# Four-layer graph kernel on one core: layer 2 scores from stacked halves through DRAM, layer 3 attention normalised early, centred weights, and 64-column pair products

## The reference

```python
# layer 0, hypergraph convolution, twice, with relu and layer norm between them
H = (adj != 0); xw = x @ W.T
m = Be[:, :, None] * einsum('nce,nch->neh', H, xw)       # Be: 1 / column count of H
out = Dn[:, :, None] * einsum('nce,neh->nch', H, m) + b  # Dn: 1 / (H @ first row of adj)
# layer 1
agg = einsum('bij,bjd->bid', adj, k * mask)
w = mask / 16 * einsum('bid,bid->bi', q, agg)
L = softmax(w, axis=1)[:, :, None] * v
# layer 2, eight heads of 32
scores = einsum('bhqd,bhkd->bhqk', q, k) * SCALE * (adj + adj)
out = einsum('bhqk,bhkd->bhqd', softmax(scores), v) @ Wo.T + bo
# layer 3
xg = x * sigmoid(deg * Wd + bd); QK = sigmoid(xg @ Wqk.T + bqk)
scores = einsum('bnd,bmd->bnm', QK, QK) / 16 * adj
attn = scores / (scores.sum(-1) + 1e-6)
out = relu((attn @ xg) @ Wl.T + bl + xg @ Wr.T)
```

## Time and profile before

| | |
|---|---|
| median of three runs | 999.5 us (997.31 to 1002.46) |
| the profiled execution's own time | 999.49 us |
| its span, first to last instruction | 997.7 us |
| TensorE busy | 928.4 us, 93% |
| VectorE busy | 836.6 us, 84% |
| GpSimd busy | 746.0 us, 75% |
| ScalarE busy | 702.5 us, 70% |
| mean granted TensorE clock | 0.977 of full |
| DMA | 61.80 MB, 23.4% of 16 engines' span |

### The profile page before, as it was taken

One profiled execution on the slowest core, in us unless ns is written; L12 is line 12 of the kernel. 1 busy time (PEld: TensorE's weight loads), 2 busy tenths in 40 slices (PEclk: granted clock), 3 DMA queues, 4 the chain that ended last, 5 costly groups with the idle time before them and its releaser, 6 DMA issues. The chain is left out here.

```text
span 997.7 us, 32479 instructions
## 1 busy us (share of the span) xinstructions
PE 928.4 (93%) x11228; PEld 812.0 (81%) x11228; DVE 836.6 (84%) x2503; ACT 702.5 (70%) x1516; POOL 746.0 (75%) x1169
## 2 busy tenths in 40 slices
PE   4687899999999999999999999999999999999854
PEld 3566788888888888888888888888888888887642
DVE  4467888898998999899988899899989898988752
ACT  3445667777777777877787777787787777776552
POOL 2655768878878888888888888888888888876551
PEclk9779999999999999999999999999999999999995
DMA  7102221222222222222222222222222222212200
GB/s 238 40 9 60 58 68 50 56 54 61 71 71 71 56 68 53 58 61 61 71 71 71 59 66 56 56 59 65 68 71 71 63 63 67 54 37 52 52 20 21
DMA packets 110231, 61.80 MB, mean 62 GB/s; under 512 B 57072, under 2 KB 105840, under 8 KB 110192
## 3 DMA queue, kind: packets, MB, share of 16 engines
q1 hardware_dynamic: 110192, 61.30, 23.4%
HBM read 35.83 MB, written 8.39 MB: 44 GB/s over the span
## 5 line engine op out<-in xcount | busy, mean ns | idle before, releaser
L784 ACT ACTIVATE late<-preG,nbG,rsG 128x256 f32<-128x256 f32 x64 | 34.9, 592 | 63.1 <-POOL nbG L1295 63.1
L481 PE MATMUL bank<-z1h,W 128*128 128x256 f16 x256 | 72.0, 281 | 3.8 <-DVE z1l L951 3.6
L482 PE MATMUL bank<-z1l,W 128*128 128x256 f16 x256 | 72.0, 281 | 0.0
L483 PE MATMUL bank<-z1h,W 128*128 128x256 f16 x256 | 72.0, 281 | 0.0
L1374 POOL TENSOR_TENSOR late<-late,Smx 128x512 f32<-128x512 f32 x64 | 67.5, 1055 | 4.7 <-DVE Smx L1182 4.7
L481 PE MATMUL bank<-W,rFh 128*128 128x256 f16 x256 | 70.7, 276 | 0.0
L483 PE MATMUL bank<-W,rFl 128*128 128x256 f16 x256 | 70.7, 276 | 0.0
L482 PE MATMUL bank<-W,rFh 128*128 128x256 f16 x256 | 70.7, 276 | 0.0
L1300 POOL TENSOR_TENSOR gp<-late,bdb 128x512 f32<-128x512 f32 x32 | 40.7, 1271 | 32.7 <-ACT late L897 32.7
L813 ACT ACTIVATE r<-bank,b1c 128x256 f32<-128x256 f32 x128 | 52.6, 463 | 16.7 <-PE bank L483 16.7
L1283 POOL TENSOR_TENSOR y0l<-y,y0h 128x512 f16<-128x512 f32 x32 | 37.2, 1163 | 31.6 <-ACT y0h L766 31.6
(11 more groups left out here) (286 smaller groups left out, 4519.0 us busy)
## 6 DMA issues: line engine op xcount, KB each, us to landing
Vbd<-vst SPq DMA_DIRECT2D x128, 66.0 KB, 2.1
xin<-x SPq DMA_DIRECT2D x32, 256.0 KB, 2.7
xres<-x SPq DMA_DIRECT2D x32, 256.0 KB, 2.9
Kbd<-kst SPq DMA_DIRECT2D x128, 64.0 KB, 2.0
out<-late SPq DMA_DIRECT2D x32, 256.0 KB, 2.2
mrow<-mask SPq DMA_DIRECT2D x32, 128.0 KB, 3.1
atA<-adj_t SPq DMA_DIRECT2D x64, 32.0 KB, 2.3
aC<-adj SPq DMA_DIRECT2D x64, 32.0 KB, 2.1
```

The source lines that it names most:

```text
L481: pe.matmul(o, sh, mh, start=start, stop=False, skip_group_check=True)
L482: pe.matmul(o, sh, ml, start=False, stop=False, skip_group_check=True)
L483: return pe.matmul(o, sl, mh, start=False, stop=stop, skip_group_check=True)
L784: m = act.activation(dst[:, t], pre[k][:, t], ACT.Identity, bias=nb[k][:, t:t + 1], scale=rs[k][:, t:t + 1])
```

## The change

- Layer 2's scores contract over 96 rows: a head's q is stacked as (high, high, low) and its k as (high, low, high), so that one product of 64 columns per head, tile and graph gives all three parts. The stacking moves rows between partitions: q and k are written to a DRAM scratch and read back in three parts. SyncE's list gets `park_k` at the head of the step, `fetch_k` after `load_residual`, and `park_q`, `store`, `fetch_q` at the end. `Kbd` and its clearing go.
- Layer 3's attention is normalised before it meets y3: VectorE sums each row while it multiplies by adj, GpSimd scales the rows, TensorE turns the matrix, ScalarE and VectorE split it, and the bias, xg Wr and the attention product all accumulate in one bank; VectorE then takes relu and adds the residual in one instruction.
- Layers 1 and 3 compute only the diagonal 64 x 64 blocks, and `am`, the mask and `atG` are 64 columns wide.
- Wv1, Wo and bo are centred in the set-up so that two norms (C and F) have mean zero and need no mean product.
- The second half of the `rF` remainder moves from VectorE to GpSimd. All order lists are new.

```diff
-ORDER_PE = [3, 2, 1, 5, 0, 2, 4, 4, 3, 2, 5, 1, 0, 2, 0, 4, 3, 5, 0, 0, 3, 1, 5, 4, 5, 1, 3, 2, 5, 3, 1, 0, 2, 0, 4]
+ORDER_PE = [1, 2, 3, 5, 3, 0, 4, 4, 2, 1, 2, 0, 5, 4, 0, 2, 5, 3, 3, 0, 1, 0, 4, 5, 1, 2, 5, 3, 5, 2, 3, 1, 0, 0, 4]
-ORDER_ACT = [0, 5, 2, 3, 5, 1, 3, 0, 4, 5, 0, 0, 4, 4, 1, 4, 0, 5, 0, 0, 1, 0, 0, 2, 0, 3, 1, 3, 2, 5, 4, 3, 2, 4, 5]
+ORDER_ACT = [3, 1, 5, 5, 0, 2, 0, 4, 0, 3, 5, 4, 0, 4, 4, 1, 1, 0, 0, 0, 2, 5, 3, 0, 0, 2, 0, 1, 3, 4, 3, 2, 4, 5]
-ORDER_DVE = [0, 2, 0, 0, 2, 0, 0, 0, 0, 4, 1, 3, 4, 0, 4, 0, 2, 4, 4, 2, 5, 1, 0, 1, 3, 1, 5, 0, 2, 2, 2, 5, 3, 4, 3, 3, 3, 1, 5, 4, 0, 4, 5, 4, 5, 1, 5, 2, 1, 0, 3, 0, 5, 5, 1, 0, 3, 2, 4]
+ORDER_DVE = [0, 0, 0, 1, 0, 2, 0, 2, 0, 4, 3, 0, 4, 0, 0, 4, 4, 4, 1, 2, 5, 0, 1, 2, 3, 1, 5, 0, 4, 2, 5, 2, 5, 3, 2, 3, 5, 1, 3, 4, 3, 5, 4, 4, 2, 1, 5, 1, 5, 3, 0, 5, 0, 2, 0, 3, 1, 4]
...
-            def place_k(at):
+            def park(name, dram, at):
+                sp.dma_start(dram[at.par].rearrange("l p k -> p l k"),
+                             (qst if name == "q" else kst)[:].rearrange("p l c k -> p l (c k)")
+                             ).then_inc(ev(name + "_parked"), 16)
+            def fetch(name, dram, dst, parts, at):
+                sp.wait_ge(ev(name + "_parked"), at.chain(16, 16)).then_inc(ev("sp_held"), 1)
+                for r, hl in enumerate(parts):
+                    sp.dma_start(dst[32 * r:32 * r + 32].rearrange("p a c k -> p a (c k)"),
+                                 dram[at.par][hl].rearrange("(a p) k -> p a k", p=32)
+                                 ).then_inc(ev(name + "_stacked"), 16)
...
+                    park_k(at)
                 for k, load in enumerate(loads):
                     at = At(k, j, s + 1)
-                    if load and there(at):
+                    if load and k != 5 and there(at):
                         load(at)
+                    at = At(3, j, s)
+                    if k == 1 and there(at):
+                        fetch_k(at)
...
+                pe.wait_ge(ev("q_stacked"), at.chain(48, 48))
+                pe.wait_ge(ev("k_stacked"), at.chain(48, 48))
...
-                        for i, (qq, hl) in enumerate(((qh, 0), (qh, 1), (ql, 0))):
+                        for a in range(4):
                             for b in range(2):
...
-                                m = pe.matmul(o[64 * b:64 * b + 64, c * 256:(c + 1) * 256], qq[:, c, tok],
-                                              Kbd[:, :, hl, c, tok], start=(i == 0), stop=(i == 2),
+                                m = pe.matmul(o[64 * b:64 * b + 64, h * NODES:(h + 1) * NODES],
+                                              Qs[:, at.par, a, c, tok], Ks[:, a, c, tok], start=True, stop=True,
...
+                for b in range(2):
                     for k in range(2):
+                        for i, (qa, qb) in enumerate(((Qh, Qh), (Qh, Ql), (Ql, Qh))):
+                            for t in range(TILES):
...
+                pe.transpose(bG[:, D + P:2 * D], SAs[:].rearrange("p b k -> p (b k)"), ident[:]
...
+                pe.matmul(bG[:].rearrange("p (t d) -> p t d", t=TILES), ones16[:, 0:1].broadcast_to([P, P]),
+                          blr[:].rearrange("p (o d) -> p o d", o=1).broadcast_to([P, TILES, D]), start=True, stop=False,
...
-                for t in range(TILES):
-                    m = mm3(bG[:, t * D:(t + 1) * D], SAh[:, t], SAl[:, t], y3h[:, t], y3l[:, t], True, True)
+                for t in range(TILES):
+                    for i, (sa, y) in enumerate(((SAh, y3h), (SAh, y3l), (SAl, y3h))):
+                        for b in range(2):
+                            rows = slice(64 * b, 64 * b + 64)
+                            m = pe.matmul(bG[rows, t * D:(t + 1) * D], sa[rows, t], y[rows, t], start=False,
...
+                dve.scalar_tensor_tensor(out=pre["G"][:].rearrange("p t k -> p (t k)"), in0=bG[:], scalar=0.0,
+                                         in1=x3[:, at.par].rearrange("p t k -> p (t k)"), op0=ALU.max, op1=ALU.add
```

More of the change, by code:

```diff
@@ L453, in step @@
                     place_v(at)
+                at = At(5, j, s + 1)
+                if there(at):
+                    load_layer3(at)
+                at = At(2, j, s)
+                if there(at):
+                    park_q(at)
                 at = At(5, j, s)
@@ L456, in step @@
                     store(at)
+                at = At(2, j, s)
+                if there(at):
+                    fetch_q(at)
             first = LAST_LAG + 1
@@ L716, in stream4 @@
                 if at.earlier(1):
-                    pe.wait_ge(ev("mixed"), at.n(-1))
+                    pe.wait_ge(ev("preG"), at.n(-1))
                 turn(bG, xg).then_inc(ev("xg_turned"), 1)
@@ L733, in stream5 @@
                 pe.wait_ge(ev("Q_lo"), at.n())
[L734 to L735 removed]
+                for b in range(2):
                     for k in range(2):
[L737 removed]
+                        for i, (qa, qb) in enumerate(((Qh, Qh), (Qh, Ql), (Ql, Qh))):
+                            for t in range(TILES):
+                                tok = slice(t * P + 64 * b, t * P + 64 * b + 64)
+                                m = pe.matmul(bG[64 * t:64 * t + 64, D + b * NODES:D + (b + 1) * NODES], qa[:, k, tok],
+                                              qb[:, k, tok], start=(k == 0 and i == 0), stop=(k == 1 and i == 2),
+                                              skip_group_check=True)
@@ L977, in part, with centre @@
                     low(W[:, 1], split_from[name], W[:, 0], WS).then_inc(ev("unstaged"), 1)
+                def centre(rows, sums, done):
+                    dve.tensor_reduce(wmean[:, sums], rows, AX.X, ALU.add).then_inc(ev("centring"), 1)
+                    dve.wait_ge(ev("centring"), done + 1)
+                    dve.tensor_scalar(wmean[:, sums], wmean[:, sums], -1.0 / D, None, ALU.mult
+                                      ).then_inc(ev("centring"), 1)
+                    dve.wait_ge(ev("centring"), done + 2)
+                    for i in range(rows.shape[1]):
+                        k = sums.start + i
+                        m = dve.tensor_scalar(rows[:, i], rows[:, i], wmean[:, k:k + 1], None, ALU.add)
+                    m.then_inc(ev("centring"), 1)
                 dve.wait_ge(ev("w2_in"), 64)
@@ L1009, in set_up @@
                 m.then_inc(ev("setup"), 1)
+                dve.tensor_scalar(blr[:], blf[:], WS, None, ALU.mult).then_inc(ev("bl_row"), 1)
+                dve.wait_ge(ev("bl_row"), 1)
+                low(blr[32:33], blf[32:33], blr[32:33], WS).then_inc(ev("bl_row"), 1)
                 yield
-                for i in range(2, 7):
+                part(2)
+                yield
+                dve.wait_ge(ev("second_in"), 32)
+                centre(stages["Wv1"], slice(0, 2), 0)
+                yield
+                part(3)
+                yield
+                dve.wait_ge(ev("rest_in"), arrival("Wo")[1])
+                centre(stages["Wo"], slice(2, 4), 3)
+                yield
+                centre(bob[:].rearrange("p (o d) -> p o d", o=1), slice(4, 5), 6)
+                yield
+                for i in range(4, 7):
                     part(i)
@@ L1246, in stream5 @@
                 yield
-                dve.wait_ge(ev("o1"), at.n())
-                dve.wait_ge(ev("row_scale"), at.chain(2, 2))
-                if at.earlier(1):
-                    dve.wait_ge(ev("o3_relu"), at.n(-1))
-                for t in range(TILES):
-                    m = dve.scalar_tensor_tensor(out=o3[:, t], in0=bG[:, t * D:(t + 1) * D], scalar=srec[:, t:t + 1],
-                                                 in1=o2[:, t], op0=ALU.mult, op1=ALU.add)
-                m.then_inc(ev("mixed"), 1)
+                dve.wait_ge(ev("attn_hi"), at.n())
@@ L1270, in set_up @@
             def set_up():
-                for h in range(4):
-                    pool.memset(Kbd[:, h], 0.0).then_inc(ev("ident"), 1)
-                    yield
                 for par in range(2):
```

264 lines of the change are left out of this document (139 added, 125 removed).

## The result

The changed kernel takes 1074.9 us (median of 4 runs, 1072.64 to 1078.89), the kernel before 998.4 us (994.25 to 1002.46) beside it. The ratio is 1.077 (95% interval 1.072 to 1.083): slower, as forecast, but by 76 us where 25 were predicted, and outside the range of 978 to 1045. The profiled executions say the same: a span of 1072.7 us against 997.7.

A forecast was written before the change was run, and what follows sets the result against it. TensorE, busy all 27.98 us of a steady step, bounds the kernel; K's longer trip makes the step 28.75. 25 steps x 0.77 = +19, fill +4.5, drain +1.5 give +25, say 1025 us; range 978 to 1045.

The forecast's parts named there:

- The new wait: TensorE's layer 2 scores wait for K's fetch from DRAM once per step: 1.8 us, as a sign 1 to 2.5.
- K there: K's arrival after the trip through DRAM, forecast at 13.9 us into the step, with TensorE at the scores at 12.1.
- T: End of K's remainder on VectorE, forecast at 5.8 us into the step, 7.0 before.
- Parking to fetch: On SyncE's queue, issue of K's parking copy to its first fetch: near 4 us with the x loads in it.
- the landing: K's fetches back from DRAM: issued 0.63 us apart, each landing after 2.6, bounds 2.0 and 2.9.
- TensorE's own sum: TensorE's work per step changes by -1.00 us, which alone makes a step of 27.0.
- Pairs of 64 columns: TensorE's paired 64-column products in layer 1 and the scores: 0.032 us per pair, halves running together.
- Fill and drain: Shorter steps at start and end of the kernel: fill +4.5 us, drain +1.5.
- Rival A: K arrives in time and TensorE's sum decides: 25 x -1.0, -2 in fill and drain, 972 us; chance 0.25.
- Rival C: Row-half y3 products on TensorE run one after the other: +0.65 x 31 = +20, 1045 us; chance 0.15.
- the 0.65: Attention times y3 on TensorE: twelve half-height products take 0.65 us side by side, 1.31 one after the other.
- The 14.9: TensorE's work behind the start of the layer 2 scores, 27.0 - 12.1 = 14.9 us, all queued behind the wait.

The follow-up runs named there:

- the two kernels without the wait: Changed kernel with two Ks buffers, scores reading K of the group before: 965.5 us; changed kernel with K's fetch directly behind its parking, ahead of the loads: 970.7 us.

## Why the prediction was right and wrong

**Right: the mechanism.** The new wait stands where the forecast put it, once a step, at 2.05 us (1.8 said, 1 to 2.5 as the bound). Its terms, counted from the start of the step, which with the new list is the first product of y0 at 506.70: layer 3 scores done at 12.2 (12.1), K there at 14.3 (13.9). T, the end of K's remainder, is 6.0 (5.8):

```profile
506.70 0.27 PE L521 MATMUL bank<-W,rFh 128*128 128x256 f16 x1
511.88 0.86 DVE L1014 SCALAR_TENSOR_TENSOR kst<-bank,bkc,kst 128x256 f16<-128x256 f32 x2
```

Parking to fetch is 3.74 and 4.11 in turn (4.2 - 0.24 = 3.96). Two terms of the landing were off and partly cancel: three issues 0.43 apart, not 0.63, and 3.5 us for the last fetch, not 2.6, of which 0.6 to 0.9 is xres in front of it. Its bounds were a 64 KB copy's 2.0 and the median of 2.9 of xres; behind another load it lies above both.

**Right: TensorE's own sum.** 27.0 was forecast for the step without a wait; it is 26.80. Pairs of 64 columns cost 0.032, both tiles' scores 0.62 from 520.97 to 521.59 with the switches. Fill and drain +4.8 (+6). Rival A's 972 is near what the two kernels without the wait took, 965.5 and 970.7. Moving the other engines' work cost nothing in the steady step, as TensorE is full in both.

**Rival C did not come.** TensorE's row-half products, each line two instructions on different row halves:

```profile
531.55 0.30 PE L809 MATMUL bank<-y3h,SAh 64*64 64x256 f16 x2
531.68 0.27 PE L809 MATMUL bank<-y3l,SAh 64*64 64x256 f16 x2
...
532.12 0.27 PE L809 MATMUL bank<-y3h,SAl 64*64 64x256 f16 x2
532.32 0.28 PE L521 MATMUL bank<-x2Fh,Wq 128*128 128x256 f16 x1
```

Pairs start 0.11 to 0.13 apart, twelve products in 0.77 us with the switch behind them, so the halves run side by side, as the 0.65 assumed. The rule of the Trainium skill weighed in the prediction (TensorEngine Tiling, Restrictions and Gotchas), that different row tiles cannot access one PSUM bank at the same time, did not show for this product, whose two row tiles write the two row halves of the same columns of one bank; the measurement decides.

**Wrong: one step.** "So the step is 13.9 plus what TensorE has behind the start of the scores, 27.0 - 12.1 = 14.9: 28.75 us". The 14.9 were priced with rows taken at the full clock, in a kernel that never pauses there. Behind the pause of 2 us the first part runs at 1.2 GHz in every step, so the pause is paid, and then 1.7 to 1.8 more. The step is 30.68, 1.93 above the forecast: 1.83 beside the pause, +0.25 pause, -0.2 work, and rounding. 26 x 1.93 = 50 us is the whole miss. The profile of before could have raised the question, as the page's clock row and the windows give the granted clock, and the forecast argued a new pause on TensorE in every step while it kept the clock of a kernel without one. The range had no case for it. The Trainium skill has it as a rule (TensorE: Matmul & The Clock Gate, HAM oscillation — how this bites in real kernels): a loop that waits for a DMA in each tile can drop to the lower clock in each; this trace agrees, with 0.51 behind the pause and the fall in each of the 20 steps from 200 to 800 us.

**Where the gain went.** The change is worth 27.98 - 26.80 = 1.2 us a step. K's trip, by the loads placed in it, turned that into a pause of 2.05 and a clock loss of 1.7, with 0.1 beside them that is open. Open: how much of the 0.2 to 0.4 that the runs with a short pause have beyond work and pause (27.54 - 26.80 - 0.53 = 0.21 with x and adj_t between; 28.92 - 26.80 - 1.74 = 0.38 with K's remainder earlier) is the restart of TensorE's queue and how much other small waits.

## What to carry to other kernels

A wait that appears on a full TensorE is priced twice: its own length, and, once it nears 2 us, the clock of what follows (1.7 us here, in every step or in most). Before a two-leg trip is added, the list of the issuing queue is to be read as part of it: each load between the legs costs its issue, and a big one also delays the landing of what stands behind it. Where only the second leg is late, moving its issue ahead of loads that nobody waits for is worth trying first; here it turned 1074.9 us into 970.7.

## What the runs showed of the hardware that was not expected

- Behind waits of TensorE for K of 1.69 us and more its granted clock mostly fell to 0.50, for 3.4 us and now and then 6.8. Between 200 and 800 us it fell behind 20 of 20 in the changed kernel (1.69 to 2.61), 19 of 19 with two more loads in the trip (2.43 to 3.27), 13 of 19 in the kernel before with a pause (2.43 to 2.75), and 2 of 3 with acD in the trip (1.90 and 2.26, not 1.91). Behind waits of 1.6 us and less it stayed at 1.00, 18 of 18 in that last run.
- The lower level began 0.3 to 1.0 us after TensorE went on in the changed kernel, and in some steps of the longer trip before it went on.
- A load of 256 KB queued directly ahead lengthened a following fetch of 128 KB pieces from 2.7 to 3.5 us, and one queued behind a parked copy lengthened that copy from 2.44 to 2.70 (issue to issue, means).
- SyncE issued copies of 32 partitions 0.43 us apart from DRAM to SBUF, and 0.63 apart from SBUF to SBUF.
